# The fourth gate chunk ahead of C's row for state 11 on TensorE, and all residuals added by GpSimd

## The chip, the cores and the metric

The kernel runs on one core of a Trainium2 chip. The metric is the time of one execution on the device in microseconds. A profile of one execution shows what each engine did in it: TensorE (PE, its weight loads PEld), VectorE (DVE), ScalarE (ACT), GpSimd (POOL) and SyncE (SP), which issues the transfers.

## The reference

The block has a state-space layer (Mamba's selective scan) that is gated by a second input, and a feed-forward layer with ternary weights behind it. Shapes: x (4, 512, 512), ctx (4, 512, 256), 16 states, F = 2048.

```python
# scan part: u = silu(conv(in_proj(ctx))), dt = softplus(...), B, C = rows of x_proj(u)
def step(state, inp):
    d, b, c, u = inp
    dA = jnp.exp(d[..., None] * A)
    state = state * dA + (d * u)[..., None] * b[:, None, :]
    y = jnp.einsum('bdn,bn->bd', state, c)
    return (state, y)
...
y = y + D[None, :, None] * x
y = y * silu(z)                       # z = layernorm(x)
...
x = x + jnp.tanh(g_xattn[0]) * _L0_xattn_ref(ctx_1024, _layernorm(x, axis=-1), ...)
x = x + jnp.tanh(g_ffn[0]) * _L0_ffn_ref(_layernorm(x, axis=-1), ...)
# ffn: gate = silu(bitlinear(x, w_gate)); up = bitlinear(x, w_up); bitlinear(gate * up, w_down)
# bitlinear: rmsnorm, activations rounded to 8 bits per token, weights rounded to -1, 0, 1
```

## The kernel before

The scan's work is cut into 16 tiles s (4 batches of 4 blocks of 128 channels, 512 time steps along the free axis). For each tile and each of the 16 states n, ScalarE computes exp(dt * A) into a PSUM bank (`exponential`, line 1001), VectorE scans it (`scan`, line 1314) with dt * u * B, which GpSimd made (`times_b`, line 755, two states at a time, four buffers), and the result is multiplied by C's row. For eight states VectorE does this (`times_c`, line 1322) with C's row that TensorE has spread over a PSUM bank (`c_bcast`, line 437); for the other four pairs GpSimd does (`times_c`, line 747). TensorE transposes the products and adds them up in the bank pY (`y_sum` and `y_sum_pooled`, line 443). When the tile's sum is complete, VectorE multiplies it by the gate (`gated_y`, line 1333), which happens in the next step behind scan 2. The residual adds x to that (`residual`): line 725 on GpSimd, line 1327 on VectorE.

The feed-forward layer is cut into 16 token tiles t. It is woven into the scan four tiles later: in step s the gate and up products of tile t1 = s - 4 run, the transposes and part of the down product of tile t2 = s - 5, the rest for t3 = s - 6. For a token tile TensorE computes four gate chunks of 512 columns and then four up chunks (`gate`, `up`, line 486), in two banks pG in turn. ScalarE applies SiLU to each gate chunk (`gate_silu`, line 959), VectorE multiplies by the up chunk (`times_up`, line 1273). A bank can only be overwritten when SiLU has read it: gate chunk c waits for the SiLU of chunk c - 2.

No scheduler is at work. Each engine has its instructions written out in order, and semaphores tie the engines together. In step s the ScalarE queue holds exponential 13, then SiLU of chunks 0 and 1, the SiLU of z of the next tile, SiLU of chunks 2 and 3, and only then exponential 14. The VectorE queue holds scan 12, product of state 10, scan 13, the output of tile t3, product of state 11, product of the first up chunk, scan 14.

Semaphores of the places that change: `c_bcast(s, n)` waits for the product before it (`s_mul`), since C's rows share one bank. `times_c` waits for C's row (`s_cb`). GpSimd's `residual` waits for the gated product (`s_y`) and for x from memory, and it signals `s_x1`, which the load of x two tiles on, the gate's next copy and the statistics of the finished batch wait for.

Of the kernel before, what the change touches and what calls it, by code (L numbers as in the profile page):

```python
# [8 lines left out]
ALU = mybir.AluOpType  # L9
# [10 lines left out]
NT = D // P  # L20
# [30 lines left out]
def own(s):  # L51
    return [n for n in range(NS) if n // CH not in pooled(s)]
# [10 lines left out]
def own_stats(t):  # L63

    return t % NT == 0 or t >= UNITS - NT


def own_residual(s):

    return s % NT == 2 and s >= NT  # L70

# [18 lines left out]
def past(eng, sem, value):  # L92

    if value > 0:
        eng.wait_ge(sem, value)


def carve(area, at, cols, dt=F32):
    v = area[:, at:at + cols]
    return v if dt == F32 else v.bitcast(dt)  # L100


def build(nc, x, ctxT, g_x, g_f, w_in, w_conv, b_conv, w_xp, w_dt, b_dt, a_log, d_skip, w_gate, w_up, w_down,
          bc_rows, u_rows, out):
    with ExitStack() as stack:
        def sb(name, shape, dt=F32):
            return stack.enter_context(nc.sbuf_tensor(name, shape, dt))
# [5 lines left out]
        dt_all = sb("dt_all", [P, UNITS, L])  # L113
# [30 lines left out]
        szT = sb("szT", [P, NT * P])  # L144
# [28 lines left out]
        xr = [carve(area_s, 9728 + L * i, L) for i in range(2)]  # L173
# [23 lines left out]
        S = {n: stack.enter_context(nc.semaphore(n)) for n in SEMAPHORES}  # L197
# [13 lines left out]
        def gate_bank(c):  # L211
            return pG[c % 2][:, :]
# [13 lines left out]
        def c_bank(s, m):  # L226
            return pC[:, m % 2 if s < PLAIN else 0, :]
# [127 lines left out]
        def _(pe):  # L355
# [76 lines left out]
            def c_bcast(s, n):  # L432
                m = own(s).index(n)

                past(pe, S["s_mul"], OWN_AT[s] + m - (1 if s < PLAIN else 0))
                for k in range(NT):
                    mm = pe.transpose(c_bank(s, m)[:, k * P:(k + 1) * P],  # L437
                                      xdT[:, s // NT, k, NS + n:NS + n + 1].to_broadcast([P, P]), ident[:, :])
                mm.then_inc(S["s_cb"], 1)
# [20 lines left out]
            def y_skip(s):  # L460

                if s >= PLAIN:
                    pe.wait_ge(S["s_y"], s)
                pe.wait_ge(S["s_skip"], s + 1)
                y_part(du_skip, first=(s >= PLAIN)).then_inc(S["s_skd"], 1)
# [17 lines left out]
            def gate_up(t, c, m, bank):  # L483

                for k in range(NT):
                    mm = pe.matmul(bank, xqT[t % 2][:, k, :], wq_gu[:, k, m, c * GW:(c + 1) * GW], start=(k == 0), stop=(k == NT - 1))  # L486
                mm.then_inc(S["f_up" if m else "f_gate"], 1)

            def gate(t, c):
                if c < 2:  # L490
                    pe.wait_ge(S["f_xqT"], t + 1)
                    past(pe, S["f_hqT"], HR * t)
                else:
                    pe.wait_ge(S["f_silu"], FC * t + c - 1)
                gate_up(t, c, 0, gate_bank(c))
# [40 lines left out]
            def fill(s, first, last):  # L536

                for part in range(first, last):
                    if s - NT - 2 >= 0:
                        down(s - NT - 2, part, s)  # L540
                    else:
                        keep_on(s)
# [27 lines left out]
            for s in range(PLAIN, UNITS):  # L570
                t1, t2 = s - NT, s - NT - 1
                fill(s, 0, 1)
                if s > PLAIN:
                    y_sum(s - 1, 15)
                    y_sum_pooled(s - 1, 3)
                c_bcast(s, 2)
                fill(s, 1, 2)
                y_skip(s)
                y_sum(s, 2)
                c_bcast(s, 3)  # L580
                fill(s, 2, 4)
                if t1 % NT:
                    pe.wait_ge(S["f_h"], FC * t1)
                    xq_transpose(t1, pG[0])
                y_sum(s, 3)
                c_bcast(s, 6)
                y_sum_pooled(s, 0)
                if t2 >= 0:
                    if t1 % NT:
                        pe.wait_ge(S["f_xqT"], t1 + 1)  # L590
                    hq_transpose(t2, 0, pG)
                    hq_transpose(t2, 1, pG)
                fill(s, 4, DPARTS)
                if t2 >= 0:
                    hq_transpose(t2, 2, pG)
                    hq_transpose(t2, 3, pG)
                y_sum(s, 6)
                c_bcast(s, 7)
                if t1 % NT == 0:
                    past(pe, S["f_h"], FC * t1)  # L600
                    past(pe, S["f_hqT"], HR * t1 - 1)
                    xq_transpose(t1, pG[0])
                gate(t1, 0)
                gate(t1, 1)
                y_sum_pooled(s, 1)
                y_sum(s, 7)
                c_bcast(s, 10)
                gate(t1, 2)
                c_bcast(s, 11)
                gate(t1, 3)  # L610
                y_sum(s, 10)
                up(t1, 0)
                up(t1, 1)
                z_transpose(s)
                y_sum(s, 11)
                y_sum_pooled(s, 2)
                c_bcast(s, 14)
                if s < UNITS - 1:
                    up(t1, 2)
                    up(t1, 3)  # L620
                    y_sum(s, 14)
                    c_bcast(s, 15)

            s, t = UNITS - 1, UNITS - NT
# [56 lines left out]
        def _(gp):  # L681
# [40 lines left out]
            def residual(s):  # L722
                gp.wait_ge(S["s_y"], s + 1)
                gp.wait_ge(S[f"d_xr{s % 2}"], (s // 2) * 16 + 16)
                gp.tensor_tensor(dt_all[:, s, :], szT[:, :], xr[s % 2], ALU.add).then_inc(S["s_x1"], 1)
# [59 lines left out]
            for s in range(PLAIN, UNITS):  # L785
                t1, t2 = s - NT, s - NT - 1
                times_b(s, NDB)
                if t2 >= 0:
                    h_rstd(t2)
                if not own_residual(s - 1):  # L790
                    residual(s - 1)
                times_c(s, 0)
                times_b(s, NDB + 1)
                times_b(s, NDB + 2)

                if t1 % NT == 0:
                    x_rstd(t1)
                if t1 % NT and (t1 + 1) % NT:
                    x_rstd(t1 + 1)
                times_c(s, 1)  # L800
                times_b(s, NDB + 3)
                if s + 1 < UNITS:
                    dt_u(s + 1)
                    times_b(s + 1, 0)
                if t1 % NT == 0:
                    x_rstd(t1 + 1)
                times_c(s, 2)
                if s + 1 < UNITS:
                    times_b(s + 1, 1)
                    times_b(s + 1, 2)  # L810
                times_c(s, 3)
                if s + 1 < UNITS:
                    times_b(s + 1, 3)
# [337 lines left out]
        def _(dve):  # L1151
# [169 lines left out]
                past(dve, S["s_ytr"], i - NH + 1)  # L1321
                dve.tensor_tensor(p_st[i % NH], h_st[i % NH], c_bank(s, m), ALU.mult).then_inc(S["s_mul"], 1)  # L1322

            def residual(s):
                dve.wait_ge(S["s_y"], s + 1)
                dve.wait_ge(S[f"d_xr{s % 2}"], (s // 2) * 16 + 16)
                dve.tensor_tensor(dt_all[:, s, :], szT[:, :], xr[s % 2], ALU.add).then_inc(S["s_x1"], 1)  # L1327

            def gated_y(s):
                dve.wait_ge(S["s_ytr"], OWN_AT[s + 1])  # L1330
                dve.wait_ge(S["s_pytr"], POOLED_AT[s + 1])
# [16 lines left out]
            for s in range(PLAIN, UNITS):  # L1348
                t1, t2, t3 = s - NT, s - NT - 1, s - NT - 2
                for n in range(NS):  # L1350
                    scan(s, n)
                    if n == 0 and s > PLAIN:
                        times_c(s - 1, 15)
                    if n == 13 and t3 >= 0:
                        output(t3)
                    for state, step in C_STEP.items():
                        if step == n:
                            times_c(s, state)
                    if n == 2:
                        gated_y(s - 1)  # L1360
                    if n == 3 and own_residual(s - 1):
                        residual(s - 1)
                    if n == 3 and t2 >= 0:
                        h_max(t2)
                    if n == 4 and t2 >= 0:
                        h_scales(t2)
                    if n == 4 and t1 % NT == 0:
                        stats(t1)
                    if n == 7 and t1 % NT == 0:
                        x_scales(t1)  # L1370
                    if n == (11 if t1 % NT else 13) and (t1 + 1) % NT:
                        x_scales(t1 + 1)
                    if n in (13, 14, 15):
                        times_up(t1, n - 13, gate_bank(n - 13))
                if s < UNITS - 1:
                    times_up(t1, 3, gate_bank(3))


            s, t = UNITS - 1, UNITS - NT
# [84 lines left out]
```

## Time and profile before

| what | value |
|---|---|
| time, median of 3 runs | 646.54 us (644.51 to 647.14) |
| time of the profiled execution | 646.37 us |
| its span, first to last instruction | 644.6 us |
| mean granted TensorE clock, share of full speed | 0.958 |
| DVE busy | 572.3 us |
| POOL busy | 518.2 us |
| ACT busy | 512.0 us |
| PE busy | 509.4 us |

The profiled execution is the source of all rows below. Its own time lies 1.8 us above its span, and 0.2 us below the median of the runs. Steps 4 to 15, in which both layers run together, take up the stretch from about 184 us to 577 us.

### The profile page before, as it was taken

To read this page: it belongs to the slowest core of one execution; us is meant where nothing else is said; L and a number is where in the kernel's file an instruction comes from. 1 tells how busy PE (TensorE), PEld (TensorE's weight loads), DVE (VectorE), ACT (ScalarE), POOL (GpSimd) and SP (SyncE) were. 2 spreads that over 40 slices of the span, in tenths; PEclk is the share of its full clock that TensorE was granted. 3 is DMA by queue.
4 is the path that set the end of the run, shared out by engine and by line. 5 is a ranking of instruction groups with operands and counts; after the bars stand their busy time and mean duration, and the time that the engine had idled before them with its cause. 6 is when DMAs were issued, how large, how long until landed. Compare 5 with 4: busy or idle time off the path is not lost. (4 is left out here: it accounts for less than half of the span.)

```text
span 644.6 us, 9211 instructions
## 1 busy us (share of the span) xinstructions
PE 509.4 (79%) x3014; PEld 345.8 (54%) x3014; DVE 572.3 (89%) x780; ACT 512.0 (79%) x761; POOL 518.2 (80%) x283
## 2 busy tenths in 40 slices
PE   6999575766768787869768787878677878799997
PEld 2443364755665565537545555565455555564553
DVE  2899989999988989999999999999989999987664
ACT  4869699787968888859698888787889797678784
POOL 2568899999989899988998999979989999731100
PEclk9999778888878999998999999989999999899999
DMA  9991921712820101118300010075111110000001
GB/s 293 399 413 63 376 81 33 262 49 77 341 73 1 49 2 34 34 46 325 121 17 23 28 40 27 34 284 173 34 33 34 34 34 17 1 16 18 18 16 50
DMA packets 29985, 64.47 MB, mean 100 GB/s; under 512 B 3681, under 2 KB 11873, under 8 KB 26866
## 3 DMA queue, kind: packets, MB, share of 16 engines
q1 hardware_dynamic: 29938, 63.89, 27.4%
q8 instruction: 24, 0.39, 0.3%
q14 instruction: 23, 0.19, 0.1%
HBM read 55.75 MB, written 8.13 MB: 99 GB/s over the span
## 5 line engine op out<-in xcount | busy, mean ns | idle before, releaser
L755 POOL TENSOR_TENSOR area_s<-area_s,b_bc 128x1024 f32<-128x1024 f32 x128 | 302.3, 2373 | 28.2 <-DVE u_all L1314 23.2
L443 PE MATMUL pY<-ident,area_s 128*128 128x128 f32 x640 | 104.9, 290 | 91.9 <-DVE area_s L1322 85.8
L443 PEld LDWEIGHTS pY<-ident,area_s 128*128 128x128 f32 x640 | 73.0, 145 | 127.5 <-DVE area_s L1322 91.4
L1001 ACT ACTIVATE pA<-dt_all,a_neg 128x512 f32<-128x512 f32 x160 | 107.7, 682 | 23.5 <-DVE area_s L1314 12.5
L1314 DVE TENSOR_TENSOR_SCAN area_s<-pA,area_s 128x512 f32<-128x512 f32 x96 | 114.4, 1206 | 8.2 <-ACT pA L1001 8.2
L486 PE MATMUL pG<-wq_gu,area_f 128*128 128x512 fp8e4 x448 | 109.2, 382 | 7.7 <-ACT area_f L953 3.6
L747 POOL TENSOR_TENSOR u_all<-u_all 128x1024 f32<-128x1024 f32 x44 | 103.9, 2361 | 0.2 <-DMA u_all<-bc_rows 0.2
L1322 DVE TENSOR_TENSOR area_s<-area_s,pC 128x512 f32<-128x512 f32 x144 | 95.5, 665 | 6.6 <-issue 4.4
L437 PE MATMUL pC<-ident,xdT 128*128 128x128 f32 x576 | 91.6, 287 | 7.3 <-DVE area_s L1322 6.6
L437 PEld LDWEIGHTS pC<-ident,xdT 128*128 128x128 f32 x576 | 71.5, 146 | 13.1 <-DVE area_s L1322 11.1
L486 PEld LDWEIGHTS pG<-wq_gu,area_f 128*128 128x128 bf16 x448 | 41.8, 98 | 51.4 <-ACT area_f L959 6.1
L526 PE MATMUL pT<-wq_dn,area_f 128*128 128x512 fp8e4 x240 | 59.4, 380 | 0.0
L1314 DVE TENSOR_TENSOR_SCAN u_all<-pA,area_s 128x512 f32<-128x512 f32 x48 | 57.8, 1212 | 0.1
L443 PE MATMUL pY<-ident,u_all 128*128 128x128 f32 x352 | 52.1, 297 | 1.7 <-POOL u_all L747 1.7
L1001 ACT ACTIVATE pC<-dt_all,a_neg 128x512 f32<-128x512 f32 x64 | 43.7, 683 | 9.9 <-DVE u_all L1314 6.6
L443 PEld LDWEIGHTS pY<-ident,u_all 128*128 128x128 f32 x352 | 45.9, 155 | 4.7 <-POOL u_all L747 2.1
L959 ACT ACTIVATE area_f<-pG,area_f 128x512 f32<-128x512 f32 x52 | 34.4, 685 | 15.8 <-PE pG L486 15.0
L736 POOL TENSOR_TENSOR area_f<-area_f,neg_half 128x1 f32<-128x1 f32 x16 | 8.8, 552 | 44.9 <-ACT area_f L969 33.7
L1314 DVE TENSOR_TENSOR_SCAN area_s<-pC,area_s 128x512 f32<-128x512 f32 x32 | 38.6, 1206 | 4.5 <-ACT pC L1001 4.5
L1273 DVE TENSOR_TENSOR area_f<-area_f,pG 128x512 f32<-128x512 f32 x52 | 34.4, 678 | 7.6 <-PE pG L486 5.8
L700 POOL TENSOR_TENSOR area_s<-area_s 128x511 f32<-128x511 f32 x16 | 20.1, 1278 | 20.8 <-DVE area_s L1161 20.8
L517 PE MATMUL pG<-ident,area_f 128*128 128x128 f32 x176 | 26.0, 294 | 10.6 <-ACT area_f L992 10.6
(198 smaller groups left out, 985.9 us busy)
## 6 DMA issues: line engine op xcount, KB each, us to landing
b_bc<-bc_rows SPq DMA_DIRECT2D x16, 1024.0 KB, 9.0
area_s<-x SPq DMA_DIRECT2D x32, 256.0 KB, 2.9
u_all<-bc_rows SPq DMA_DIRECT2D x14, 512.0 KB, 5.9
b_bc<-w_gate SPq DMA_DIRECT2D x1, 4096.0 KB, 15.1
dt_all<-x SPq DMA_DIRECT2D x1, 4096.0 KB, 25.4
area_f<-w_up SPq DMA_DIRECT2D x1, 4096.0 KB, 34.8
area_f<-w_down SPq DMA_DIRECT2D x1, 4096.0 KB, 15.1
out<-area_f SPq DMA_DIRECT2D x16, 256.0 KB, 2.0
```

Source lines behind the costliest of these rows:

```text
L437: mm = pe.transpose(c_bank(s, m)[:, k * P:(k + 1) * P], xdT[:, s // NT, k, NS + n:NS + n + 1].to_broadcast([P, P]), ident[:, :])
L443: mm = pe.matmul(pY[:, k * P:(k + 1) * P], src[:, k * P:(k + 1) * P], ident[:, :], is_transpose=True, start=(first and k == 0), stop=(last ...
L486: mm = pe.matmul(bank, xqT[t % 2][:, k, :], wq_gu[:, k, m, c * GW:(c + 1) * GW], start=(k == 0), stop=(k == NT - 1))
L517: mm = pe.transpose(banks[r % 2][:, k * P:(k + 1) * P], h_of(t)[:, (4 * r + k) * P:(4 * r + k + 1) * P], ident[:, :])
L526: mm = pe.matmul(pT[:, :], hqT[t % 2][:, k, :], wq_dn[:, k, :], start=(k == 0), stop=(k == FK - 1))
L747: gp.tensor_tensor(hp[j], hp[j], c_bc[j], ALU.mult).then_inc(S["s_pmul"], 1)
L755: gp.tensor_tensor(db[c % NDB], du[s % 2].rearrange("p (a l) -> p a l", a=1).to_broadcast([P, CH, L]), b_bc[:, CH * c:CH * c + CH, :], ALU ...
L959: act.activation(h_of(t)[:, c * GW:(c + 1) * GW], bank, ACT.Silu, scale=col(CS[t % 2])).then_inc(S["f_silu"], 1)
L1001: act.activation(exp_bank(s, n), dt_all[:, s, :], ACT.Exp, scale=a_neg[:, s % NT, n:n + 1]).then_inc(S["s_exp"], 1)
L1273: dve.tensor_tensor(chunk, chunk, bank, ALU.mult).then_inc(S["f_h"], 1)
L1314: dve.tensor_tensor_scan(h, exp_bank(s, n), db[(n // CH) % NDB][:, n % CH, :], 0.0, ALU.mult, ALU.add).then_inc(S["s_scan"], 1)
L1322: dve.tensor_tensor(p_st[i % NH], h_st[i % NH], c_bank(s, m), ALU.mult).then_inc(S["s_mul"], 1)
```

## The change

On TensorE the fourth gate chunk of tile t1 (`gate(t1, 3)`, four matmuls) and C's row for state 11 (`c_bcast(s, 11)`, four transposes) change places in each of the steps 4 to 15. The residuals of tiles 6, 10 and 14, which VectorE added in steps 7, 11 and 15, are added by GpSimd like all others. Nothing else is changed; in the program, later line numbers are a few lines lower.

```diff
-def own_residual(s):
-
-    return s % NT == 2 and s >= NT
...
                 y_sum(s, 7)
                 c_bcast(s, 10)
                 gate(t1, 2)
+                gate(t1, 3)
                 c_bcast(s, 11)
-                gate(t1, 3)
                 y_sum(s, 10)
                 up(t1, 0)
                 up(t1, 1)
...
                 if t2 >= 0:
                     h_rstd(t2)
-                if not own_residual(s - 1):
-                    residual(s - 1)
+                residual(s - 1)
                 times_c(s, 0)
                 times_b(s, NDB + 1)
                 times_b(s, NDB + 2)
...
-            def residual(s):
-                dve.wait_ge(S["s_y"], s + 1)
-                dve.wait_ge(S[f"d_xr{s % 2}"], (s // 2) * 16 + 16)
-                dve.tensor_tensor(dt_all[:, s, :], szT[:, :], xr[s % 2], ALU.add).then_inc(S["s_x1"], 1)
...
                     if n == 2:
                         gated_y(s - 1)
-                    if n == 3 and own_residual(s - 1):
-                        residual(s - 1)
                     if n == 3 and t2 >= 0:
                         h_max(t2)
```

TensorE's order in step 5, before, from the first pair of gate chunks (L486 is gate and up, L443 the sums, L437 C's rows, L474 the transpose of the gate z):

```order
L486 MATMUL pG<-wq_gu,area_f 128x512 x8
L443 MATMUL pY<-ident,u_all 128x128 x8
L443 MATMUL pY<-ident,area_s 128x128 x4
L437 MATMUL pC<-ident,xdT 128x128 x4
L486 MATMUL pG<-wq_gu,area_f 128x512 x4
L437 MATMUL pC<-ident,xdT 128x128 x4
L486 MATMUL pG<-wq_gu,area_f 128x512 x4
L443 MATMUL pY<-ident,area_s 128x128 x4
L486 MATMUL pG<-wq_gu,area_f 128x512 x8
L474 MATMUL pT<-ident,zt 128x128 x4
```

And the same place of the changed kernel, whose lines stand five lower (L481 is gate and up, L438 the sums, L432 C's rows):

```order
L481 MATMUL pG<-wq_gu,area_f 128x512 x8
L438 MATMUL pY<-ident,u_all 128x128 x8
L438 MATMUL pY<-ident,area_s 128x128 x4
L432 MATMUL pC<-ident,xdT 128x128 x4
L481 MATMUL pG<-wq_gu,area_f 128x512 x8
L432 MATMUL pC<-ident,xdT 128x128 x4
L438 MATMUL pY<-ident,area_s 128x128 x4
L481 MATMUL pG<-wq_gu,area_f 128x512 x8
L469 MATMUL pT<-ident,zt 128x128 x4
```

Gate chunks 2 and 3 now follow each other as eight matmuls, and C's row for state 11 comes behind both.

VectorE's order in step 7, before, from the scan of state 1 (L1314 is a scan, L1333 the gated product, L1322 a product with C's row, L1327 the residual, L1277 the maximum over the hidden tile):

```order
L1314 SCALAR_TENSOR_TENSOR u_all<-pA,area_s 128x512
L1314 SCALAR_TENSOR_TENSOR area_s<-pC,area_s 128x512
L1333 TENSOR_TENSOR szT<-pY,szT 128x512
L1314 SCALAR_TENSOR_TENSOR area_s<-pA,area_s 128x512
L1322 TENSOR_TENSOR area_s<-area_s,pC 128x512
L1327 TENSOR_TENSOR dt_all<-szT,area_s 128x512
L1277 TENSOR_REDUCE area_f<-area_f 128x1
```

The same place in the changed kernel (L1308 is a scan, L1322 the gated product, L1316 a product with C's row, L1271 the maximum):

```order
L1308 SCALAR_TENSOR_TENSOR u_all<-pA,area_s 128x512
L1308 SCALAR_TENSOR_TENSOR area_s<-pC,area_s 128x512
L1322 TENSOR_TENSOR szT<-pY,szT 128x512
L1308 SCALAR_TENSOR_TENSOR area_s<-pA,area_s 128x512
L1316 TENSOR_TENSOR area_s<-area_s,pC 128x512
L1271 TENSOR_REDUCE area_f<-area_f 128x1
```

The addition is gone from VectorE; GpSimd has one more in its place between its inverse root and its first product with C's row.

## Rows read from the trace of the kernel before

**Rows 1.** The page: busy time, share and instructions of each engine.
```profile
PE 509.4 (79%) x3014; PEld 345.8 (54%) x3014; DVE 572.3 (89%) x780; ACT 512.0 (79%) x761; POOL 518.2 (80%) x283
```

**Rows 2.** VectorE in order of time: start, duration, line; gated products, steps 6 to 8.
```profile
248.87 0.67 DVE L1333 TENSOR_TENSOR szT<-pY,szT 128x512 f32<-128x512 f32 x1
...
280.93 0.67 DVE L1333 TENSOR_TENSOR szT<-pY,szT 128x512 f32<-128x512 f32 x1
...
314.27 0.67 DVE L1333 TENSOR_TENSOR szT<-pY,szT 128x512 f32<-128x512 f32 x1
```

**Rows 3.** VectorE and GpSimd in order of time, around the residual of step 7.
```profile
283.22 2.56 DVE L1327 TENSOR_TENSOR dt_all<-szT,area_s 128x512 f32<-128x512 f32 x1
285.71 2.27 DVE L1277 TENSOR_REDUCE area_f<-area_f 128x1 f32<-128x2048 f32 x1
...
282.88 2.36 POOL L747 TENSOR_TENSOR u_all<-u_all 128x1024 f32<-128x1024 f32 x1
285.18 2.81 POOL L755 TENSOR_TENSOR area_s<-area_s,b_bc 128x1024 f32<-128x1024 f32 x1
291.65 2.37 POOL L755 TENSOR_TENSOR area_s<-area_s,b_bc 128x1024 f32<-128x1024 f32 x1 [3.66 <-DVE u_all L1314]
```

**Rows 4.** GpSimd's residuals, one line: count, then ns minimum/median/maximum.
```profile
L725 POOL TENSOR_TENSOR dt_all<-szT,area_s x12: 1254/1270/1278, 102.3 to 516.6; 128x512 f32<-128x512 f32 x12
```

**Rows 5.** Order of time in step 6: TensorE, ScalarE, VectorE around the gate chunks.
```profile
265.93 1.04 PE L486 MATMUL pG<-wq_gu,area_f 128*128 128x512 fp8e4 x4
268.02 0.65 PE L437 MATMUL pC<-ident,xdT 128*128 128x128 f32 x4 [1.05 <-DVE area_s L1322]
...
265.18 1.26 ACT L959 ACTIVATE area_f<-pG,area_f 128x512 f32<-128x512 f32 x2
...
269.62 0.69 ACT L959 ACTIVATE area_f<-pG,area_f 128x512 f32<-128x512 f32 x1 [1.88 <-PE pG L486]
...
269.65 0.68 DVE L1322 TENSOR_TENSOR area_s<-area_s,pC 128x512 f32<-128x512 f32 x1
270.87 0.69 DVE L1273 TENSOR_TENSOR area_f<-area_f,pG 128x512 f32<-128x512 f32 x1 [0.54 <-PE pG L486]
272.35 1.22 DVE L1314 TENSOR_TENSOR_SCAN area_s<-pA,area_s 128x512 f32<-128x512 f32 x1 [0.79 <-ACT pA L1001]
```

**Rows 6.** Order of time in step 7, same place.
```profile
301.40 0.61 PE L437 MATMUL pC<-ident,xdT 128*128 128x128 f32 x4
301.85 1.03 PE L486 MATMUL pG<-wq_gu,area_f 128*128 128x512 fp8e4 x4
...
302.96 0.69 ACT L959 ACTIVATE area_f<-pG,area_f 128x512 f32<-128x512 f32 x1 [0.62 <-PE pG L486]
...
303.00 0.68 DVE L1322 TENSOR_TENSOR area_s<-area_s,pC 128x512 f32<-128x512 f32 x1
...
305.68 1.22 DVE L1314 TENSOR_TENSOR_SCAN area_s<-pC,area_s 128x512 f32<-128x512 f32 x1 [0.78 <-ACT pC L1001]
```

**Rows 7.** VectorE in order of time in step 8, same place.
```profile
337.53 0.69 DVE L1322 TENSOR_TENSOR area_s<-area_s,pC 128x512 f32<-128x512 f32 x1 [0.76 <-issue]
...
339.64 0.69 DVE L1273 TENSOR_TENSOR area_f<-area_f,pG 128x512 f32<-128x512 f32 x1
341.12 1.22 DVE L1314 TENSOR_TENSOR_SCAN area_s<-pA,area_s 128x512 f32<-128x512 f32 x1 [0.79 <-ACT pA L1001]
```

**Rows 8.** GpSimd's products and TensorE's sums of them, ends of steps 6 and 7.
```profile
257.12 2.36 POOL L755 TENSOR_TENSOR area_s<-area_s,b_bc 128x1024 f32<-128x1024 f32 x1 [0.39 <-DVE u_all L1314]
...
275.22 2.35 POOL L747 TENSOR_TENSOR area_f<-area_f,u_all 128x1024 f32<-128x1024 f32 x1
...
279.31 1.04 PE L443 MATMUL pY<-ident,area_f 128*128 128x128 f32 x8
...
309.23 2.36 POOL L747 TENSOR_TENSOR area_f<-area_f,u_all 128x1024 f32<-128x1024 f32 x1
...
312.66 1.04 PE L443 MATMUL pY<-ident,area_f 128*128 128x128 f32 x8
```

## The prediction

> **What bounds the kernel now.** I read the page first, then the order of events of every engine around one tile, because no engine is full and shares say little. VectorE is busy for 89% of the span, GpSimd 80%, TensorE and ScalarE 79% [rows 1]. Tiles 4 to 15 take a step each, and the steps differ by their place in a batch of four. I call s = 5, 6, 9, 10, 13, 14 middle steps, s = 7, 11, 15 closing steps and s = 4, 8, 12 opening steps. The gated product, once a step, gives the period: the step before the row at 280.93 took 32.06 us, the closing one behind it 33.34 us [rows 2]. All three closing steps hold a residual on VectorE.
>
> In the order of events VectorE runs without a gap for most of a step. The exception is the place where the four gate chunks pass through SiLU. There it waits in a middle step 0.54 us for the first up chunk and 0.79 us for the exponential of state 14 [rows 5], and a closing step has the second wait too [rows 6]. GpSimd's own waits are for VectorE's scans (3.66 us in a closing step [rows 3], 0.39 us in a middle one [rows 8]). So the chain runs along VectorE, and at that place through TensorE and ScalarE. The change touches both.
>
> **The residuals.** Three additions leave VectorE. The one at 283.22 took 2.56 us, and the next operation began at 285.71, so each holds VectorE for 2.49 us [rows 3]. Nothing waits for its result at once, and the maximum behind it needs only data of the step before. The time is thus taken off the chain: 3 x 2.49 = 7.5 us. GpSimd gets three more additions of 1.27 us, the median of its twelve [rows 4]. Its place is ahead of the product at 282.88, where the gated product (280.93 plus 0.67) is already done. Behind that place GpSimd had waited 3.66 us for a scan [rows 3], so 1.27 us fits in. SyncE's load of x two tiles on waits for the residual, with the next batch's loads queued behind it. The new residual ends at about 284.2, not at 285.8, so these don't get later. If that cover were gone, the cost would be 3.8 us in all.
>
> The nearest rule speaks against this move. The Trainium skill ("GPSIMD Engine Reference", section 3.1) says that VectorE is about twice as fast at an elementwise operation with two tensors, and that such work belongs there. By that ratio and the 1.27 us of GpSimd, VectorE should need about 0.65 us, and three would give 1.9 us instead of 7.5 us. The trace disagrees: 2.56 us on VectorE against 1.27 us on GpSimd for the same shape. The skill's "SBUF — State Buffer", section "Who interferes with whom", offers a reason (two SBUF inputs on VectorE share a read path with GpSimd and wait for its whole instruction). The row fits it: the residual began at 283.22 inside the product that GpSimd ended at 285.24, and it ended about 0.54 us later. I take the measured 2.49 us.
>
> **The gate chunk in a middle step (six of them).** Before, gate chunk 3 stood behind C's row for state 11, and that waited 1.05 us for VectorE's product 10, until 268.02 [rows 5]. Gate chunk 2 ran 265.93 to 266.97, and the SiLU of chunk 1 that chunk 3 needs was over by 266.44. So chunk 3 now runs in the hole: at the latest 266.97 plus 1.04 = 268.01. C's row keeps its time to within some hundredths. Its SiLU, which stood idle for 1.88 us and began at 269.62, can begin at about 268.05. From the start of that SiLU to the scan of state 14 it is 2.73 us here (272.35 less 269.62) and 2.72 us in a closing step [rows 5, 6]. So that scan is allowed from 270.8. The up chunks also stand one gate chunk (0.87 us, below) earlier, so the 0.54 us wait goes. VectorE then is its own limit: product 11 from 269.65 for 0.68 us, times the up chunk for 0.69 us, which ends at 271.0. Without a wait an operation starts some 0.07 us ahead of the printed end of the one before (285.71 against 285.78 [rows 3]), so the scan starts at about 270.9. The gain is at least the two idle times, 1.33 us, and at most 272.35 less 270.8 = 1.55 us. I take 1.45 us: 6 x 1.45 = 8.7 us.
>
> **In a closing step (three).** Here C's row doesn't wait: it stands at 301.40 and the gate chunk at 301.85 [rows 6]. The exchange brings the chunk 0.45 us ahead. Its SiLU had waited 0.62 us for it, so all of that reaches the scan of state 14, which still waits: 0.44 us each, 1.3 us in all. C's row goes back by one gate chunk. A chunk lasts 1.03 us and the next instruction starts some 0.16 us ahead of a printed end (301.40 plus 0.61 against 301.85), so that is 0.87 us. C's row then ends at about 302.9, and product 11 starts at 303.00: covered, by only 0.1 us. If it came later it would first eat into the wait ahead of the scan of state 14.
>
> **In an opening step (three).** There product 11 already waits 0.76 us for C's row [rows 7], so it goes back by 0.87 us. The multiplication by the up chunk moves from 339.64 to 340.5 and ends at 341.2. The scan of state 14 stood at 341.12 after a wait of 0.79 us. The wait swallows the delay: change between 0 and 0.1 us, I take 0. Without this cover it would be 3 x 0.87 = 2.6 us.
>
> **What is late next.** GpSimd. Before, its last product of step 6 ended at 277.57 and TensorE used it at 279.31, a slack of 1.74 us [rows 8]. After two middle steps VectorE and TensorE are 2.9 us ahead. GpSimd gets back only the waits that it had, 0.39 us and a few tenths at its other stops, say 0.7 us. So TensorE comes about 2.9 - 0.7 - 1.74 = 0.5 us too early. I count 0.3 us, since VectorE reads this sum only after two more operations. In the closing step VectorE and TensorE reach 2.9 - 0.3 + 2.5 + 0.4 = 5.5 us. GpSimd reaches 0.7 + 3.66 - 1.27 = 3.1, and 0.45 us more, because the product that took 2.81 us beside VectorE's residual [rows 3] goes back to 2.36: 3.6 us. The slack at the same place is 312.66 - 311.59 = 1.07 us [rows 8], so 0.8 us is missing; I count 0.5 us. The opening step lets GpSimd catch up. This costs 0.8 us for the first two batches. In the last, step 15 has no next tile for GpSimd, so only the 0.3 us stays: 1.9 us in all.
>
> **The sum.** 7.5 + 8.7 + 1.3 - 1.9 = 15.6 us. The profiled execution took 646.37 us (its span 644.6 us), the median of the runs is 646.54 us: 0.2 us apart. That gives 646.4 - 15.6 = 630.8 us. The stretch behind step 15 starts when VectorE is through and moves as a whole.
>
> **Rivals.**
> - *GpSimd takes the chain over.* If all its products are tied to TensorE more tightly than the two pairs that I read, the middle steps yield only its 0.7 us per batch: 2.1 + 7.5 + 1.3 = 10.9 us, so 635.5 us. For it: twelve products of some 2.36 us a step leave it little room. Against it: 3.66 us of wait in each closing step. Chance 0.10.
> - *C's row comes too late.* If the later row delays VectorE by the whole 0.87 us in opening and closing steps: 6 x 0.87 = 5.2 us less, so 636.0 us. The waits right behind it speak against that. Chance 0.05.
> - *The residual is cheap.* The time VectorE gives up appears as a wait at the next scan, and only 1.9 of the 7.5 us stay, which is also where the skill's ratio ("GPSIMD Engine Reference", above) would lead: 636.4 us. The middle steps, which run the same sequence without that addition and without a wait, speak against it. Chance 0.04.
> - *Slower.* GpSimd is the limit in closing steps and each added 1.27 us goes through, while the gate chunk's gain is hidden behind it: 646.4 + 3.8 = 650.2 us. It decides once GpSimd's wait at 291.65 is below 1.27 us; it is 3.66 us. Chance 0.03.
> - *No effect.* Both waits return elsewhere in the step, 646.4 us. Chance 0.03.
>
> My forecast has 0.75. The range reaches from 627.5 us (no loss to GpSimd, 1.55 us in each middle step: 628.0, with half a microsecond of spread) to 636.5 us. It leaves out the last two cases and some of the first. A measurement tells a difference from no change at about 0.5%, 3.2 us. Faster by more than that 0.94, within it 0.03, slower 0.03.
>
> **What the new profile should show.** No VectorE addition behind state 3 and 15 on GpSimd of about 1.27 us. Middle steps of about 30.6 us and closing steps of about 30.4 to 31 us instead of 32.06 and 33.34, opening steps as before. No wait ahead of the first up product in middle steps; in closing steps the wait for the exponential of state 14 down from 0.78 to about 0.35 us; in opening steps that for C's row up from 0.76 to about 1.6 us. TensorE waits for GpSimd's products by some tenths at the end of closing steps. I am wrong if GpSimd shows no wait for scans any more, if TensorE's waits for GpSimd reach a microsecond per step, or if the closing steps stay above 32 us.

## The result and the profile after

The changed kernel takes 629.66 us (median of 4 runs, 629.21 to 630.89) against 645.61 us (median of 4 runs, 644.51 to 647.14) of the kernel before: a ratio of 0.9754, 95% interval 0.9726 to 0.9783. The profiled execution took 629.84 us, 16.5 us less than that of before; its span is 628.0 us. The forecast was 630.8 us, range 627.5 to 636.5. It took 15.6 us off 646.4 us, and the medians differ by 15.95 us; the start was 0.8 us too high, since the median of before, now with a fourth run, is 645.61 us.

The page's first row, to be read against [rows 1]. VectorE lost 7.8 us of busy time, while its share hardly moved. GpSimd's share rose from 80% to 83%.

```profile
PE 506.1 (81%) x3014; PEld 340.5 (54%) x3014; DVE 564.5 (90%) x777; ACT 511.8 (81%) x761; POOL 520.1 (83%) x286
```

VectorE in order of time: the gated products of steps 6, 7 and 8, as in [rows 2]. The middle step that ends at the second row took 30.93 us, the closing one behind it 30.92 us, where they had been 32.06 and 33.34 us. The waits of 0.20 us are new.

```profile
246.64 0.67 DVE L1322 TENSOR_TENSOR szT<-pY,szT 128x512 f32<-128x512 f32 x1
...
277.57 0.69 DVE L1322 TENSOR_TENSOR szT<-pY,szT 128x512 f32<-128x512 f32 x1 [0.20 <-issue]
...
308.49 0.69 DVE L1322 TENSOR_TENSOR szT<-pY,szT 128x512 f32<-128x512 f32 x1 [0.20 <-issue]
```

Order of time in a middle step, the place of [rows 5]. The gate chunks 2 and 3 are now one row of eight matmuls, and C's row behind them still begins when VectorE's product 10 is through: its wait shrank from 1.05 to 0.18 us. The SiLU of chunk 3 waits 0.18 us instead of 1.88. Product 11, the multiplication by the first up chunk and the scan of state 14 follow each other on VectorE without any wait. From product 11 to that scan it is now 268.62 - 267.43 = 1.19 us, where it was 2.70.

```profile
263.70 1.90 PE L481 MATMUL pG<-wq_gu,area_f 128*128 128x512 fp8e4 x8
265.79 0.65 PE L432 MATMUL pC<-ident,xdT 128*128 128x128 f32 x4 [0.18 <-DVE area_s L1316]
...
265.69 0.69 ACT L953 ACTIVATE area_f<-pG,area_f 128x512 f32<-128x512 f32 x1 [0.18 <-PE pG L481]
...
267.43 0.68 DVE L1316 TENSOR_TENSOR area_s<-area_s,pC 128x512 f32<-128x512 f32 x1
268.02 0.68 DVE L1267 TENSOR_TENSOR area_f<-area_f,pG 128x512 f32<-128x512 f32 x1
268.62 1.22 DVE L1308 TENSOR_TENSOR_SCAN area_s<-pA,area_s 128x512 f32<-128x512 f32 x1
```

VectorE in the closing step, the place of [rows 6], with C's row for state 11 on TensorE behind it, then VectorE in the opening step, the place of [rows 7]. In the closing step the wait for the exponential of state 14 fell from 0.78 to 0.35 us. Product 11 has a wait of 0.17 us there, for which the trace names no releaser. It isn't C's row: that had ended at 296.99, 0.45 us earlier, and in the closing steps 11 and 15 product 11 starts without a wait. In the opening step the wait for C's row grew from 0.76 to 1.63 us, and the one ahead of the scan of state 14 is gone.

```profile
297.44 0.69 DVE L1316 TENSOR_TENSOR area_s<-area_s,pC 128x512 f32<-128x512 f32 x1 [0.17 <-issue]
298.33 0.69 DVE L1267 TENSOR_TENSOR area_f<-area_f,pG 128x512 f32<-128x512 f32 x1 [0.20 <-PE pG L481]
299.37 1.22 DVE L1308 TENSOR_TENSOR_SCAN area_s<-pC,area_s 128x512 f32<-128x512 f32 x1 [0.35 <-ACT pC L995]
...
296.39 0.60 PE L432 MATMUL pC<-ident,xdT 128*128 128x128 f32 x4
...
332.76 0.69 DVE L1316 TENSOR_TENSOR area_s<-area_s,pC 128x512 f32<-128x512 f32 x1 [1.63 <-issue]
...
335.37 1.22 DVE L1308 TENSOR_TENSOR_SCAN area_s<-pA,area_s 128x512 f32<-128x512 f32 x1
```

Between GpSimd and TensorE ([rows 8] of before) the slack is used up. TensorE waits 0.55 us for GpSimd's last product at the end of both steps 6 and 7. GpSimd itself waits for a scan at 224.43, and then not once until 343.06, which is through the two steps and most of the opening one. In step 7 TensorE also waits 0.33 us for GpSimd's third product, so 0.88 us in all.

```profile
276.39 1.09 PE L438 MATMUL pY<-ident,area_f 128*128 128x128 f32 x8 [0.55 <-POOL area_f L742]
...
307.31 1.09 PE L438 MATMUL pY<-ident,area_f 128*128 128x128 f32 x8 [0.55 <-POOL area_f L742]
...
224.43 2.37 POOL L750 TENSOR_TENSOR area_s<-area_s,b_bc 128x1024 f32<-128x1024 f32 x1 [0.38 <-DVE u_all L1308]
...
343.06 2.37 POOL L750 TENSOR_TENSOR area_s<-area_s,b_bc 128x1024 f32<-128x1024 f32 x1 [1.55 <-DVE u_all L1308]
```

### The profile page after: what moved, and what is told of

It is laid out like the page before. It is cut to its first block and busy times, and to the rows that moved or that the text cites. A ratio compares the mean times of both kernels' runs of the same rounds, so it can differ in the third digit from the quotient of the medians.

```text
span 628.0 us, 9211 instructions
## 1 busy us (share of the span) xinstructions
PE 506.1 (81%) x3014; PEld 340.5 (54%) x3014; DVE 564.5 (90%) x777; ACT 511.8 (81%) x761; POOL 520.1 (83%) x286
## 5 line engine op out<-in xcount | busy, mean ns | idle before, releaser
L438 PE MATMUL pY<-ident,area_s 128*128 128x128 f32 x640 | 104.5, 290 | 78.2 <-DVE area_s L1316 74.6
L438 PEld LDWEIGHTS pY<-ident,area_s 128*128 128x128 f32 x640 | 73.1, 145 | 109.3 <-DVE area_s L1316 78.4
L1308 DVE TENSOR_TENSOR_SCAN area_s<-pA,area_s 128x512 f32<-128x512 f32 x96 | 114.4, 1206 | 2.6 <-ACT pA L995 2.0
L481 PE MATMUL pG<-wq_gu,area_f 128*128 128x512 fp8e4 x448 | 107.8, 384 | 7.5 <-ACT area_f L953 3.5
L1316 DVE TENSOR_TENSOR area_s<-area_s,pC 128x512 f32<-128x512 f32 x144 | 95.6, 666 | 8.6 <-issue 5.7
L432 PE MATMUL pC<-ident,xdT 128*128 128x128 f32 x576 | 90.8, 285 | 1.8 <-DVE area_s L1316 1.1
L432 PEld LDWEIGHTS pC<-ident,xdT 128*128 128x128 f32 x576 | 71.2, 145 | 7.1 <-DVE area_s L1316 4.4
L481 PEld LDWEIGHTS pG<-wq_gu,area_f 128*128 128x128 bf16 x448 | 42.1, 98 | 54.1 <-ACT area_f L953 5.6
L1308 DVE TENSOR_TENSOR_SCAN u_all<-pA,area_s 128x512 f32<-128x512 f32 x48 | 57.8, 1213 | 0.0
L438 PE MATMUL pY<-ident,u_all 128*128 128x128 f32 x352 | 50.3, 290 | 3.1 <-POOL u_all L742 2.8
L438 PEld LDWEIGHTS pY<-ident,u_all 128*128 128x128 f32 x352 | 43.5, 150 | 8.1 <-POOL u_all L742 5.4
L1308 DVE TENSOR_TENSOR_SCAN area_s<-pC,area_s 128x512 f32<-128x512 f32 x32 | 38.6, 1206 | 1.7 <-ACT pC L995 1.7
L521 PEld LDWEIGHTS pT<-wq_dn,area_f 128*128 128x128 bf16 x240 | 23.5, 98 | 19.3
```

Of the source, the lines that this page charges most:

```text
L432: mm = pe.transpose(c_bank(s, m)[:, k * P:(k + 1) * P], xdT[:, s // NT, k, NS + n:NS + n + 1].to_broadcast([P, P]), ident[:, :])
L438: mm = pe.matmul(pY[:, k * P:(k + 1) * P], src[:, k * P:(k + 1) * P], ident[:, :], is_transpose=True, start=(first and k == 0), stop=(last ...
L521: mm = pe.matmul(pT[:, :], hqT[t % 2][:, k, :], wq_dn[:, k, :], start=(k == 0), stop=(k == FK - 1))
L1308: dve.tensor_tensor_scan(h, exp_bank(s, n), db[(n // CH) % NDB][:, n % CH, :], 0.0, ALU.mult, ALU.add).then_inc(S["s_scan"], 1)
```

## The experiments

The stretch ahead of step 5 differs by about a microsecond between executions of one kernel (the product that opens it begins at 216.18 us here and at 217.16 us when the same kernel was run again). So I compare the lengths of steps, from the gated product in one step to that in the next. From step 5 on they repeat to within 0.05 us where the granted clock is full. Step 4 doesn't (32.53 us here, 33.07 us when run again); the granted clock around it, from 180 to 220 us, was 0.87 in both. The times stand beside them. This table has them in us for all kernels: steps 5, 6 (middle), 7 (closing) and 8 (opening), from the profiled execution of each.

| kernel | step 5 | step 6 | step 7 | step 8 | median time |
|---|---|---|---|---|---|
| before | 32.06 | 32.06 | 33.34 | 35.43 | 645.61 |
| changed | 30.46 | 30.93 | 30.92 | 35.46 | 629.66 |
| gate chunk only | 30.46 | 30.91 | 32.00 | 35.32 | 632.76 |
| residuals only | 32.06 | 32.06 | 30.86 | 36.08 | 638.99 |
| no exchange in opening | 30.46 | 30.92 | 30.90 | 35.60 | 630.55 |
| C's row first in opening | 30.46 | 30.92 | 30.90 | 35.15 | 629.66 |
| residual twice, closing | 30.47 | 30.93 | 32.26 | 35.48 | 632.16 |
| residual twice, opening | 30.47 | 30.90 | 30.93 | 36.81 | 631.89 |
| residual from PSUM | 30.47 | 30.93 | 31.12 | 35.31 | 630.36 |
| residual twice, root early | 30.46 | 30.91 | 30.92 | 35.33 | 630.81 |
| GpSimd reordered | 30.47 | 30.60 | 30.90 | 35.31 | 628.52 |
| both reordered | 30.47 | 30.62 | 30.92 | 34.98 | 628.84 |
| changed, again | 30.46 | 30.90 | 30.93 | 35.46 | 630.48 |

**1. The gate chunk alone.** The kernel before with

```diff
                 gate(t1, 2)
+                gate(t1, 3)
                 c_bcast(s, 11)
-                gate(t1, 3)
```

> The gate chunk goes ahead of C's row as in the changed kernel, and VectorE keeps its three residuals. My theory (the chain runs along VectorE, and the middle steps yield 1.3 to 1.6 us each, the closing ones 0.44 us): 8.7 + 1.3 less 0.9 for GpSimd = 9.1 us below before, near 637 us. Rival, C's row is too late in opening and closing steps: 5.2 us less of that, near 642 us. Rival, the whole gain of the change is the residuals': near 645 us. In the trace the three VectorE residuals should still take about 2.56 us each.

It took 632.76 us against 646.51 us on the same chip (ratio 0.9795, 0.9775 to 0.9814), so 13.8 us less by the medians and 12.5 us less by the profiled executions from step 5 on (427.8 - 415.3), and not 9.1. The middle steps behave as in the changed kernel. The surprise is the closing step: 32.00 us, 1.34 us shorter than before, where I had 0.44 us for the chunk. The rows of VectorE and GpSimd in that step say why:

```profile
278.90 1.63 DVE L1327 TENSOR_TENSOR dt_all<-szT,area_s 128x512 f32<-128x512 f32 x1
280.45 2.27 DVE L1277 TENSOR_REDUCE area_f<-area_f 128x1 f32<-128x2048 f32 x1
...
275.29 4.68 POOL L755 TENSOR_TENSOR area_s<-area_s,b_bc 128x1024 f32<-128x1024 f32 x2
279.94 0.99 POOL L736 TENSOR_TENSOR area_f<-area_f,neg_half 128x1 f32<-128x1 f32 x1
```

The residual on VectorE took 1.63 us instead of 2.56 ([rows 3]). GpSimd's product beside it ended at 279.97, and the residual 0.56 us after that, as it ended 0.54 us after GpSimd's product before. GpSimd's next small operation took 0.99 us instead of the 0.55 us that it takes elsewhere. The residual's price was the rest of whatever GpSimd was doing when it came. With VectorE ahead of GpSimd by the middle steps' gain, it came at another point of GpSimd's queue, and the rest was shorter by 0.93 us. 0.44 and 0.93 make the 1.34 us within 0.03. The expectation took 2.56 us for a constant, and that was its error.

**2. The residuals alone.** The changed kernel with `gate(t1, 3)` put back behind `c_bcast(s, 11)`.

> The three residuals go to GpSimd and TensorE's order stays as before. My theory: 3 x 2.49 = 7.5 us below before, near 638.5 us; closing steps of 30.85 us, middle steps of 32.06 as before. Rival, the residual is cheap (VectorE waits elsewhere): 1.9 us, near 644 us. Rival, GpSimd is the limit: the closing steps keep 33.3 us or more and the time stays at 646 us or above. The two parts together gave 16.0 us; if this one and the gate chunk alone sum to more, the difference is what GpSimd takes back when both are in.

638.99 us, 7.5 us less than 646.51 by the medians (ratio 0.9891, 0.9870 to 0.9912). The closing step fell by 2.48 us to 30.86, as expected, and the middle steps kept 32.06. So the 2.49 us of one residual are real, and GpSimd's added 1.27 us costs nothing where VectorE isn't ahead. One opening step here has 36.08 us; the granted clock was 0.85 and 0.81 in the two stretches of 5 us ahead of the late C's row (320 to 330 us), so I don't read it as an effect of the edit. From step 5 on the two parts alone give 12.5 us and 7.5 us (6.8 with that step in), together 16.0. The difference of 4.0 us has two main causes, which the steps separate: 0.93 us of each of the three closing steps is counted in both parts (experiment 1), and in the closing steps 7 and 11 of the changed kernel GpSimd takes back 0.5 us more (experiment 5).

**3. No exchange in the opening steps.**

```diff
                 gate(t1, 2)
+                if t1 % NT == 0:
+                    c_bcast(s, 11)
                 gate(t1, 3)
-                c_bcast(s, 11)
+                if t1 % NT:
+                    c_bcast(s, 11)
```

> The changed kernel, but in the opening steps 4, 8 and 12 C's row for state 11 stays ahead of gate chunk 3. My theory: the opening steps are as long either way (35.4 us), so the time stays within 0.5 us of the changed kernel's 629.7; the wait for C's row falls from 1.63 to 0.76 us and the wait ahead of the scan of state 14 comes back with 0.79 us. Rival, the later row costs its 0.87 us in each opening step: 627.1 us.

630.55 us, opening steps of 35.60 and 35.59 against 35.46 us. The exchange is worth 0.14 us there and costs nothing. The waits on VectorE went back to 0.77 us for C's row and 0.79 us ahead of the scan of state 14, as expected. The rival that the later row costs its 0.87 us is out for opening steps, and experiment 1 rules it out for closing ones: they fell by 1.34 us with the later row in.

**4. C's row first in the opening steps.** The changed kernel with `c_bcast(s, 11)` ahead of gate chunk 2 where t1 is the first of a batch.

> The changed kernel, but in the opening steps C's row for state 11 goes ahead of gate chunks 2 and 3, into the 1.75 us in which TensorE waits for ScalarE there. My theory: VectorE then waits only for the exponential of state 14, which comes 0.44 us earlier than before the change; so each opening step loses 0.4 us and the time is 1.3 us lower, near 628.4 us. Rival, something else holds the scan of state 14 (the first up product, or ScalarE's queue): 629.7 us as the changed kernel.

The opening steps fell by 0.31 us, to 35.15 and 35.16, a little less than the 0.4 us of the theory. The time, 629.66 us, can't show it: 0.9 us is inside its own spread here (628.66 to 631.29). In this kernel the wait for C's row is gone and the two waits behind it are back, so the place is now held by ScalarE's and TensorE's chain:

```profile
332.98 0.69 DVE L1270 TENSOR_TENSOR area_f<-area_f,pG 128x512 f32<-128x512 f32 x1 [0.43 <-PE pG L481]
334.46 1.22 DVE L1311 TENSOR_TENSOR_SCAN area_s<-pA,area_s 128x512 f32<-128x512 f32 x1 [0.79 <-ACT pA L998]
```

**5 and 6. The residual twice, in closing or in opening steps.** GpSimd makes the same addition to the same place once more, in steps 7 and 11 or in steps 8 and 12:

```diff
+                if s in (6, 10):        # (7, 11) in the second kernel
+                    gp.tensor_tensor(dt_all[:, s, :], szT[:, :], xr[s % 2], ALU.add).then_inc(S["s_spare"], 1)
+                    gp.wait_ge(S["s_spare"], 1 if s < 8 else 2)
                 gp.tensor_tensor(dt_all[:, s, :], szT[:, :], xr[s % 2], ALU.add).then_inc(S["s_x1"], 1)
```

> The changed kernel, but in the closing steps 7 and 11 GpSimd makes the residual's addition twice (the first has the same inputs and place, and is waited for). In the changed kernel's trace GpSimd ran without a wait from 224.4 to 341.5 us, through steps 6 and 7 and most of the opening step. Theory that GpSimd holds the chain there: each added 1.3 us goes through, 2.6 us in all, near 632.3 us. Theory of my sum (GpSimd is short only by some tenths and VectorE's chain sets the time): it is short already, so it loses this too, but if VectorE has other cover it shows less than 1 us, near 630.5 us.

> The changed kernel, but in the opening steps 8 and 12 GpSimd makes the residual's addition twice. GpSimd waits there 1.55 us for a scan near the end of the step. Theory that GpSimd is the limit only from the first middle step on and catches up in the opening step: the added 1.3 us is swallowed by that wait, so 629.7 us, at most 0.3 us more. Rival, GpSimd is the limit everywhere: 2.6 us more, 632.3 us.

In closing steps: 632.16 us, 2.5 us above the changed kernel. The closing step grew by 1.34 us, to 32.26. All that GpSimd got more to do went through. TensorE's wait for GpSimd's first product of the step, which wasn't there, is 1.40 us now. In the changed kernel GpSimd therefore sets the length of the closing step.

```profile
286.84 1.97 PE L438 MATMUL pY<-ident,u_all 128*128 128x128 f32 x8 [1.40 <-POOL u_all L745]
```

In opening steps: 631.89 us, and step 8 grew by 1.35 us (step 12 by 1.5 us, with a granted clock of 0.70 from 451 to 456 us). My expectation of at most 0.3 us was wrong, although GpSimd has a wait of 1.56 us later in the same step. The rows of that step on VectorE and GpSimd name the link:

```profile
321.58 0.21 DVE L1257 TENSOR_SCALAR area_f<-area_f 128x1 f32<-128x1 f32 x1 [1.51 <-POOL area_f L728]
...
320.94 0.54 POOL L728 TENSOR_TENSOR area_f<-area_f,neg_half 128x1 f32<-128x1 f32 x1
```

VectorE's scale for the token tile waits 1.51 us for one number per row, the inverse root, which stands in GpSimd's queue behind three large products.

**7. The residual from PSUM on VectorE.** The changed kernel, but the residuals of tiles 6, 10 and 14 are VectorE's again, with one input in PSUM:

```diff
+                dve.tensor_tensor(pY[:, :], pY[:, :], szT[:, :], ALU.mult).then_inc(S["s_y"], 1)
+                dve.wait_ge(S["s_y"], s + 1)
+                dve.wait_ge(S[f"d_xr{s % 2}"], (s // 2) * 16 + 16)
+                dve.tensor_tensor(dt_all[:, s, :], pY[:, :], xr[s % 2], ALU.add).then_inc(S["s_x1"], 1)
```

> The changed kernel, but the residuals of tiles 6, 10 and 14 go back to VectorE, which now writes the gated product of these tiles in place into its PSUM bank and reads it there: the addition has one input in PSUM and one in SBUF. TensorE's first sum into that bank waits for it. Theory that the 2.56 us were a wait for GpSimd's instruction on a shared read path: the addition takes 0.67 us, GpSimd's products beside it stay at 2.36 us, GpSimd is relieved by 1.27 us in a closing step, and the time is within 1 us of the changed kernel's 629.7, rather below. Rival, the addition is slow by itself: 2.5 us again, 3 x 1.2 us or more above, near 634 us.

The residual on VectorE, and GpSimd's operations beside it:

```profile
277.03 0.69 DVE L1331 TENSOR_TENSOR dt_all<-pY,area_s 128x512 f32<-128x512 f32 x1
...
275.02 4.67 POOL L752 TENSOR_TENSOR area_s<-area_s,b_bc 128x1024 f32<-128x1024 f32 x2
279.65 0.55 POOL L733 TENSOR_TENSOR area_f<-area_f,neg_half 128x1 f32<-128x1 f32 x1
```

0.69 us in the midst of a GpSimd product, and neither is held up. That confirms the reading of [rows 3]: the 2.56 us were 0.6 us of work behind a wait for GpSimd's instruction, and the wait goes with the second input in SBUF. The Trainium skill ("SBUF — State Buffer", section "Who interferes with whom") says that a VectorE instruction with two inputs in SBUF contends with a GpSimd instruction that reads SBUF, and that one with at most one such input doesn't; these rows agree.

A second input in SBUF costs nothing by itself. The kernel before shows it behind step 15, where GpSimd has been idle for microseconds: the addition of 128 columns from SBUF takes as long as the product beside it that reads PSUM.

```profile
577.20 0.29 DVE L1384 TENSOR_TENSOR szT<-pY,szT 128x128 f32<-128x128 f32 x1 [0.75 <-PE pY L443]
577.53 0.29 DVE L1387 TENSOR_TENSOR dt_all<-szT,area_s 128x128 f32<-128x128 f32 x1
...
579.10 0.55 POOL L730 TENSOR_TENSOR area_f<-area_f,neg_half 128x1 f32<-128x1 f32 x1 [8.39 <-DVE area_f L1252]
```

The time, 630.36 us, is that of the changed kernel. The closing step has 31.12 us, 0.2 more, and the opening one 35.31, 0.15 less. So with the collision gone it hardly matters which engine adds.

**8. The residual twice in opening steps, the inverse root early.** As the second kernel of experiments 5 and 6, with the root one product earlier in GpSimd's queue:

```diff
                 times_b(s, NDB + 1)
+                if t1 % NT == 0:
+                    x_rstd(t1)
                 times_b(s, NDB + 2)
-
-                if t1 % NT == 0:
-                    x_rstd(t1)
```

> As the kernel that makes the residual's addition twice in the opening steps 8 and 12 (there each opening step grew by 1.35 to 1.5 us), but in the opening steps GpSimd computes the inverse root for the token tile's scale ahead of its third product of the step instead of behind it, 2.3 us earlier in its queue. Theory that the added time reached VectorE only through that inverse root (VectorE's operation behind the maximum was late by a tenth of a microsecond for it already in the changed kernel): the opening steps fall back to 35.3 to 35.5 us. Rival, GpSimd's products themselves are the limit in the opening step: 36.8 us again.

Step 8 is back at 35.33 us, with the double addition still in. So the 1.35 us went through that one small operation. Step 12 has 36.48 us, and there the granted clock fell. These are the stretches 448 to 453 us and 453 to 458 us of this kernel (columns: length, busy time of PE, PEld, DVE, ACT and POOL, granted clock, DMA share, GB/s):

```profile
448.00:453.00 5.00, 5.00 (x26) 3.91 (x25) 4.90 (x10) 4.07 (x9) 5.00 (x4) 0.59 0.00 0
453.00:458.00 5.00, 4.31 (x33) 3.17 (x32) 4.01 (x4) 4.86 (x11) 4.92 (x4) 1.00 0.02 3
```

The mean granted clock was 0.59 in the first, so TensorE ran at its lower level, 1.2 GHz, for most of it. VectorE then waited 1.35 us for C's row for state 10, where it waits 0.5 us in the changed kernel, whose clock in the same stretch is 1.00. Just before, at 446.10, TensorE had stood still for 1.39 us for GpSimd's first product, which the double addition had made late. Step 8 has the same wait (1.40 us) without a loss of time, so whether the addition had a part in the fall of the clock stays open.

**9 and 10. GpSimd's queue reordered.** The changed kernel with the root early as above, and with GpSimd's last product of the step ahead of one for the next tile. The second kernel adds C's row first in the opening steps.

```diff
                     times_b(s + 1, 1)
-                    times_b(s + 1, 2)
                 times_c(s, 3)
                 if s + 1 < UNITS:
+                    times_b(s + 1, 2)
                     times_b(s + 1, 3)
```

> The changed kernel, with two things moved in GpSimd's queue: the inverse root of the opening step one product earlier, and the last product with C's rows of every step ahead of the third product for the next tile. Theory that GpSimd is late only where TensorE reads that last product (0.55 us in steps 6 and 7): the second middle step falls from 30.85 to about 30.5 us, the closing one from 30.9 to about 30.5, the opening one from 35.46 to 35.3; 0.8 to 0.9 us a batch, near 627.5 us. Rival, GpSimd is out of time altogether in these steps: they keep 30.85 and 30.92 us, near 629.5 us.

> The same, and in the opening steps C's row for state 11 ahead of gate chunks 2 and 3. The opening steps were 0.31 us shorter with that alone; if the parts add up, 0.9 us below the reordered kernel, near 626.7 us; otherwise equal to it.

> The changed kernel as it is, beside the other three on the same chip: 629.7 us, and the same steps as before (30.5, 30.9, 30.9 and 35.5 us).

On the same chip the changed kernel took 630.48 us (630.29 to 630.76), the reordered one 628.52 us (628.07 to 629.75). Against before these are 0.9760 (0.9747 to 0.9774) and 0.9731 (0.9716 to 0.9746). The second middle step fell by 0.30 us, the opening step by 0.15 us, and the closing step did not move. The theory's 0.8 to 0.9 us a batch came to 0.45 us. In the closing step the wait only changed its place, from the last product (0.55 us) to the first (0.35 us) and the third; TensorE in order of time:

```profile
301.55 1.09 PE L438 MATMUL pY<-ident,u_all 128*128 128x128 f32 x8 [0.62 <-POOL u_all L742]
```

In the changed kernel this wait for the third product was 0.33 us. So in the closing step GpSimd is out of time altogether, in the middle one it was mostly in the wrong order. With C's row first the opening step falls to 34.98 us, so the parts add up in the steps (0.33 us more), but its time, 628.84 us, doesn't tell it from the reordered kernel. Both lie below the changed kernel by about 0.3% by the medians. For the first, the steps from 5 on account for 1.2 of the 2.0 us.

## Why the prediction was right

**The sum** was 15.6 us. From the start of step 5 to the end the profiled executions differ by 427.8 - 411.8 = 16.0 us (644.6 - 216.81 and 628.0 - 216.18). The other 0.6 us between the spans lie ahead of step 5, where executions of one kernel differ by more than that.

- *Residuals: 7.5 us.* 2.48 us in each closing step when done alone, against 2.49 us predicted. The prediction saw the wait in it and still took one fixed price, and only experiments 1 and 7 showed what it is: work of 0.6 us, and the rest of GpSimd's instruction. Beside the gate chunk it would have been 1.55 us (278.90 to 280.45). In the sum this makes no difference, since both parts are in; as an account of which part earned what it would have been wrong by 0.93 us a closing step. The prediction also set aside its estimate of 0.65 us for this addition because the trace disagreed. The work alone fits that estimate (VectorE was held from 277.03 to 277.64 in experiment 7, against 1.27 us on GpSimd); what disagreed was the wait. And the added residual ended 5.15 us behind the gated product of step 7, not 3.3 us as read from the rows of before, since GpSimd is late there; the steps show no cost of that.
- *Gate chunk in middle steps: 1.45 us each.* The first middle step of a batch gave 1.60, 1.52 and 1.51 us. The upper bound of 1.55 us was the better value: VectorE did become its own limit, with all waits there gone.
- *In closing steps: 0.44 us.* The wait for the exponential fell by 0.43 us. The cover of 0.1 us for C's row held: the row ends ahead of product 11 in all three. The wait of 0.17 us in step 7 is not for it and costs nothing, since a wait of 0.35 us follows.
- *In opening steps: 0.* Measured 0.03 us more, and 0.14 us against leaving the exchange out. The wait ahead of the scan of state 14, which the prediction named as cover, took the delay.
- *GpSimd: 1.9 us.* TensorE's computed lateness of 0.5 us at the end of the second middle step was 0.55 us. The second middle steps gave 1.13, 1.21 and 1.21 us, so GpSimd took back 0.3 to 0.5 us (0.3 predicted). The whole closing step gave 2.42 us, against 2.49 + 0.44 - 0.5 = 2.43. In all GpSimd took about 2.1 us (1.1 in the second middle steps, 0.5 in each of the steps 7 and 11). That the 1.9 us came so near is in part luck: the prediction had rounded 0.5 down to 0.3 us and 0.8 down to 0.5 us by judgement, with no row that gives either amount. The description was too mild as well. GpSimd is not short by some tenths there: it runs without a wait from 224.4 to 341.5 us and sets the step (experiment 5). The rival that GpSimd takes the chain over describes the state of steps 6 and 7 rightly; its price was too high, because GpSimd catches up in each opening step.
- *The tail.* From the last gated product in the loop to the end it is 97.9 us before and 94.9 us after: 2.49 + 0.44 us of step 15 and nothing more, so what follows moved as a whole.

**The rivals.** That C's row comes too late is refuted by experiments 3 and 1. That the residual is cheap is refuted by experiment 2. The slower case, each added 1.27 us of GpSimd going through, did not occur in this change. But experiments 5 and 6 show that one more such addition goes through: the changed kernel stands just at that point.

What would have made the forecast wrong was stated as "GpSimd shows no wait for scans any more". That nearly happened, its waits for scans fell from 23.2 to 7.3 us over the span, and the time came out right nonetheless, because the lateness was in the sum. A second sign, TensorE's waits for GpSimd reaching a microsecond per step, was just missed with 0.88 us in step 7. The third didn't appear: closing steps took 30.9 us, not above 32.

## What to carry to other kernels

A VectorE addition with both inputs in SBUF beside a busy GpSimd had no price of its own here. It cost what was left of GpSimd's instruction plus its own 0.6 us (2.56 and 1.63 us), so it changes with an edit upstream; give it to GpSimd (629.7 us) or keep one input in PSUM (630.4 us). Where engines' queues are ordered by hand, look for an engine that waits at the head for one partner while the work behind it is ready and another partner is waiting for that work; here 1.05 us of such a wait, in each of six middle steps, held up three engines. When an edit lets the leading engine run ahead, follow every queue that feeds it and compute the slack at each crossing before adding to that queue, small operations too: in the opening step one inverse root behind three products made all of GpSimd's added time count.

## What the runs showed that I had not expected

- The same VectorE addition took 2.56 us in one kernel and 1.63 us in the other, and 0.69 us with one input in PSUM.
- The two halves of the change gave 12.5 and 7.5 us alone and 16.0 us together, counted from step 5 on.
- An opening step with idle time of 1.56 us on GpSimd passed on all of 1.35 us that was added to GpSimd, because the idle time comes after the crossing that matters.
- From step 5 on the length of a step repeated to within 0.05 us when the changed kernel was run again, and single steps in other kernels came out longer where the granted clock fell (0.59 over 5 us in a step 1.15 us longer).
